# Two transformer blocks on one core: the fused loop's last stage with seven products on POOL, sums in four transfers, tokens turned a body ahead

## The chip, the cores and the metric

The kernel runs on one core of one Trainium2 chip. The metric is device time in microseconds, the median of several executions. In this text PE is the matmul engine (PEld its weight load), DVE the vector engine, ACT the scalar engine, POOL GpSimd, SP the engine that stores the output. Instructions of one engine run in the order in which they are written; engines wait for each other on semaphores.

## The reference

The input is 32 batches of 256 tokens with 128 features. Two blocks follow each other: causal attention with a mixture of experts, then hyperbolic attention with an MLP, each on a normalised input with a residual sum. The change lies in the second block alone:

```python
def _hyperbolic_distance(q, k, c):
    q_norm_sq = jnp.sum(q * q, axis=-1, keepdims=True)
    k_norm_sq = jnp.sum(k * k, axis=-1)[..., None, :]
    qk = jnp.einsum('bhnd,bhmd->bhnm', q, k)
    diff_sq = q_norm_sq + k_norm_sq - 2.0 * qk
    denom = (1.0 - c * q_norm_sq) * (1.0 - c * k_norm_sq)
    denom = jnp.maximum(denom, 1e-06)
    cosh_arg = 1.0 + 2.0 * c * diff_sq / denom
    cosh_arg = jnp.maximum(cosh_arg, 1.0)
    return jnp.arccosh(cosh_arg)
...
dist = _hyperbolic_distance(q, k, CURVATURE)     # 16 heads of 8 features
attn = jax.nn.softmax(-dist, axis=-1)
out = jnp.einsum('bhnm,bhmd->bhnd', attn, v)
return out @ wo.T
...
h = jax.nn.relu(jnp.einsum('bsd,dw->bsw', x, w1) + b1)   # the MLP, 512 wide
return jnp.einsum('bsw,wd->bsd', h, w2) + b2
```

## The kernel before

Three stages follow each other: causal attention, the mixture of experts, and the fused stage `hyperbolic_attention_and_mlp`, which has the change. The fused stage starts near 1343 us of the profiled execution and runs to the end. Its loop has one body per batch. In body b, every engine works on several batches at once: distances of batch b, softmax weights and values of batch b - 1, the back part of attention of batch b - 2, the residual and the normalisation for the MLP of batch b - 3, the MLP's products of batch b - 4 and b - 5, and the preparation of batch b + 1.

The 16 heads are taken in 8 pairs, and a body has 8 steps, one for each pair. For each pair:

- PE turns the pair's rows (`pe_turn_rows`, into `r_ps[p % 2]`), ACT (pairs 0 and 3) or DVE copies them to SBUF (`copy_rows`), and PE makes the pair products in `d_ps` and `i_ps` (`pe_pairs`). Both are single buffers, so PE makes those of the next pair only after DVE has read both.
- DVE reads `d_ps` (`dve_distances`), then `i_ps` (`dve_ratio`), and leaves u, a number from which the arccosh follows as log(1 + u + sqrt(u (u + 2))).
- For a pair in `PRODUCTS`, POOL makes u (u + 2) in `spare` (`pool_product`) and ACT takes one root. For the others, ACT takes two roots, of u/2 + 1 and of u/2 (`act_roots`).
- POOL issues a transfer that adds `spare` onto u (`pool_sum`).
- In the next body, ACT takes the logarithm and the exponential (`act_weights`), and PE multiplies with the values (`pe_values`).

The order on each engine is written out by hand in a function `body`. Step numbers in it (`VALUES_AT`, `BACK_AT`, `HIDDEN_AT` and so on) say in which step a piece stands. The first line of a step is the product of the following pair:

```python
for p in range(HP):
    following = next_pair(b, p, one_after)
    if following:
        pe_pairs(pe, *following, i if p + 1 < HP else (i + 1) % TURN)
```

`pe_keep_busy` issues matmuls whose output nobody reads; `BUSY_AHEAD` and `BUSY_BEHIND` say how many, and in which step. ACT loads one table for logarithm and exponential at the head of a body, and one for the roots behind the weights.

Of the kernel before, what the change touches and what calls it, by code (L numbers as in the profile page):

```python
# [12 lines left out]
ALU = mybir.AluOpType  # L13
# [1221 lines left out]
def hyperbolic_attention_and_mlp(nc, io, keep, y_dram, batches):  # L1235
# [11 lines left out]
    PRODUCTS = (0, 1, 2, 3, 4, 5)  # L1247
    SUMS_BEHIND = {5: (0, 1, 2, 3, 4, 5, 6, 7)}
# [5 lines left out]
    BUSY_AHEAD, BUSY_BEHIND = {5: 1}, {4: 4, 7: 1}  # L1254
    HW = WB // 2
    NORM_BEHIND, NORM4_BEHIND = 2, 5
    with ExitStack() as stack:
# [15 lines left out]
        twos = m.sb("twos", [P, 4])  # L1273
# [38 lines left out]
        sum_landed = [S_(f"sum_landed{n}") for n in range(HP)]  # L1312
# [9 lines left out]
        def wait_sum(engine, b, p):  # L1322

            after(engine, sum_landed[p], 16 * (b + 1))
# [12 lines left out]
        def pe_turn_x(pe, b):  # L1337
            pe.wait_ge(xh_done, (b + 1) * TB)
            after(pe, res_done, b - 3)
            after(pe, hi_done, b * TB)  # L1340
            after(pe, qkv_taken, b * TB)
            for j in range(TB):
                last = nc.tensor.transpose(misc[:, j * P:(j + 1) * P], xh[:, j, :], keep.ident)
            last.then_inc(xh_turned, 1)

        def pe_qkv(pe, b, j):
            pe.wait_ge(xT_done, b + 1)
            after(pe, hi_done, b * TB + j)
# [69 lines left out]

        def pe_keep_busy(count):
# [4 lines left out]
        def pe_fold_w1(pe):  # L1424
            pe.wait_ge(weights_in, 16 * 5)
            nc.tensor.matmul(o_ps[:, :], zsum[:, :], w1_rows[:, :], start=True, stop=False)
# [8 lines left out]
        def pe_hidden(pe, b, half, rows_read):  # L1435
            if half == 0:
                pe.wait_ge(w1_folded, 1)
# [27 lines left out]
        def act_xT(act, b):  # L1465
            act.wait_ge(xh_turned, b + 1)
            after(act, qkv_ready, b * TB)
            nc.scalar.copy(xTs[:, 0, :], misc[:, 0:N]).then_inc(xT_done, 1)

        def act_both_xT(act, b, b4):  # L1470
# [4 lines left out]
            nc.scalar.copy(xTs[:, :, :].rearrange("p s n -> p (s n)"), misc[:, :]).then_inc(xT_done, 1)  # L1475
# [69 lines left out]
        def pool_sum(pool, b, p, i):  # L1545
            pool.wait_ge(root_done, b * HP + p + 1)
            nc.gpsimd.dma_start(u[:, slot(i, p), :], spare[:, p, :], accum_op=ALU.add).then_inc(sum_landed[p], 16)  # L1547

        def pool_product(pool, b, p, i):
# [4 lines left out]
            nc.gpsimd.tensor_tensor(extra[:, 0:4], pair[:, 0:4], twos[:, :], ALU.add)  # L1554
            nc.gpsimd.tensor_scalar(extra[:, 4:2 * W2], pair[:, 4:2 * W2], 1.0, 2.0, ALU.mult, ALU.add).then_inc(raised, 1)  # L1555
# [149 lines left out]
        with nc.Block() as block:  # L1705
            @block.tensor
            def _(pe):
# [6 lines left out]
                pe_fold_w1(pe)  # L1714

                def body(b, i, one_before, two_before, three_before, four_before, five_before, one_after, two_after):
                    for p in range(HP):
# [30 lines left out]
                        if one_after:  # L1748
                            for r in {6: (2,), 7: (4,)}.get(p, ()):
                                pe_turn_rows(pe, b + 1, r)  # L1750
                        if one_before:
                            if p == HP - 1:
                                pe.wait_ge(o_copied, 2 * b)
                            pe_keep_busy(BUSY_BEHIND.get(p, 0))
                        if five_before and p == 0:
                            pe_y(pe, b - 5, 2 * (b - 1))
                        if four_before and p == HIDDEN_AT[0]:
                            if not one_after:
                                pe.wait_ge(late_xT4_done, 1)
# [46 lines left out]
            def _(act):  # L1806
# [284 lines left out]
```

## Time and profile before

| | us |
|---|---|
| median of 3 runs | 2449.32 (2448.59 to 2451.76) |
| profiled execution | 2456.33 |
| its span on the core | 2454.2 |
| PE, DVE, ACT, POOL busy in the span | 2089.9, 1956.8, 1767.4, 1627.2 |
| fused stage, from 1343.7 to the end | 1110.5 |
| in it DVE, ACT, POOL busy | 991.59, 1026.34, 1011.91 |

The shares of the whole span (85, 80, 72 and 66%) are means over three stages with different limits. The fused stage takes 1110.5 of the 2454.2 us, and only that part of the profile answers to the change.

### The profile page before, as it was taken

How to read it: one execution, taken by the hardware profiler on the slowest of the kernel's cores; microseconds unless marked ns; L12 is line 12 of the kernel's file. 1: busy time of each engine (PE TensorE's matmuls, PEld its weight loads, DVE VectorE, ACT ScalarE, POOL GpSimd, SP SyncE). 2: the span in 40 equal slices, each digit the busy share in tenths (PEclk: the TensorE clock that was granted, in tenths of full speed). 3: DMA queues.
4: the chain of work that ended last, by engine and by line, in shares of the span. 5: the costliest groups of instructions: out<-in, count | busy, mean ns of one | idle time of the engine just before them, and what ended most of it. 6: DMA issues, size and time to landing. Idle time of an engine off the chain costs nothing. (4 is left out here: it accounts for less than half of the span.)

```text
span 2454.2 us, 50808 instructions
## 1 busy us (share of the span) xinstructions
PE 2089.9 (85%) x15438; PEld 1566.8 (64%) x15438; DVE 1956.8 (80%) x5939; ACT 1767.4 (72%) x3085; POOL 1627.2 (66%) x1866
## 2 busy tenths in 40 slices
PE   4999999999999996999997677777777778777876
PEld 4677777777777775888885445555555555555554
DVE  4677776776777774778775899999999999999992
ACT  2666666666666762444432799999999999999996
POOL 2776676766666750000001899999999999999993
PEclk7999999999999996999997579888888988889888
DMA  5000000000000003353450466776666777666674
GB/s 142 1 2 2 2 1 2 2 1 2 1 2 1 2 2 70 86 119 76 96 114 10 93 127 130 139 138 128 124 119 127 141 141 134 119 129 124 129 142 80
DMA packets 81388, 184.24 MB, mean 75 GB/s; under 512 B 9479, under 2 KB 31530, under 8 KB 81195
## 3 DMA queue, kind: packets, MB, share of 16 engines
q0 software_dynamic: 36864, 134.23, 29.1%
q1 hardware_dynamic: 36010, 43.38, 7.9%
q10 hardware_dynamic: 8320, 4.19, 0.7%
q8 instruction: 103, 1.69, 0.3%
q14 instruction: 91, 0.74, 0.1%
HBM read 42.85 MB, written 4.72 MB: 19 GB/s over the span
## 5 line engine op out<-in xcount | busy, mean ns | idle before, releaser
L1557 POOL TENSOR_TENSOR spare<-spare,u 128x1024 f32<-128x1024 f32 x192 | 456.2, 2376 | 16.0
L542 ACT ACTIVATE prob<-s_ps,nmax 128x128 f32<-128x128 f32 (+1 forms) x1024 | 364.4, 432 | 132.2 <-DVE nmax L599 132.2
L599 DVE CUSTOM_DVE_ANT_0 s_ps<-s_ps,mask 128x128 f32<-128x128 f32 (+1 forms) x1024 | 340.7, 385 | 100.7 <-issue 76.4
L1633 DVE TENSOR_SCALAR u<-d_ps 128x1024 f32<-128x1024 f32 x256 | 312.1, 1219 | 48.7 <-PE i_ps L1374 48.1
L579 POOL TENSOR_TENSOR g_lo<-g_all,g_hi 128x512 fp32r<-128x512 f32 x256 | 329.1, 1286 | 21.4
L1637 DVE SCALAR_TENSOR_TENSOR u<-i_ps,u 128x1024 f32<-128x1024 f32 x256 | 313.5, 1225 | 13.2 <-DVE u L1633 0.5
L1374 PE MATMUL d_ps<-rowsT 28*128 28x256 f32 x1024 | 144.7, 357 | 149.5 <-DVE u L1637 145.9
L534 ACT COPY g_all<-g_ps 128x512 f32<-128x512 f32 x256 | 151.5, 592 | 162.6 <-PE g_ps L63 161.5
L1514 ACT ACTIVATE u<-u 128x1024 f32<-128x1024 f32 x256 | 257.0, 1056 | 1.7 <-DMA u<-spare 1.6
L1517 ACT ACTIVATE u<-u 128x1024 f32<-128x1024 f32 x256 | 255.7, 1051 | 0.0
L1374 PEld LDWEIGHTS d_ps<-rowsT 28*128 28x128 f32 x1024 | 92.4, 208 | 246.3 <-issue 241.7
L991 POOL TENSOR_TENSOR x_lo<-xTs,x_hi 128x512 fp32r<-128x512 f32 x16 | 21.9, 1372 | 326.8 <-ACT x_hi L987 326.8
L475 PE MATMUL t_ps<-ident,prob 128*128 128x128 f32 x1536 | 232.1, 274 | 1.6 <-ACT pT L609 1.2
L1547 POOL DMA_DIRECT2D u<-spare x256 | 228.5, 1447 | 2.0 <-ACT u L1506 1.2
L475 PEld LDWEIGHTS t_ps<-ident,prob 128*128 128x128 f32 x1536 | 192.0, 141 | 55.6 <-ACT prob L542 2.0
L1555 POOL TENSOR_SCALAR spare<-u 128x1020 f32<-128x1020 f32 x192 | 219.3, 1142 | 0.0
L1392 PE MATMUL o_ps<-u,v 128*32 128x256 f32 x2048 | 156.2, 428 | 69.9 <-ACT u L1517 69.4
L1362 PE MATMUL r_ps<-ident,rows 128*128 128x128 f32 x1024 | 186.2, 320 | 32.2 <-ACT rowsT L1494 26.4
L1159 ACT ACTIVATE act_g<-eg_ps 128x512 f32<-128x512 f32 x128 | 76.3, 598 | 189.7 <-PE eg_ps L63 189.7
L61 PE MATMUL s_ps<-g_hi,x_hi 128*128 128x512 f32 x384 | 188.6, 491 | 21.3 <-issue 17.5
L612 DVE COPY pT<-t_ps 128x512 f32<-128x512 f32 x256 | 176.7, 690 | 33.8 <-PE t_ps L475 27.5
L555 POOL TENSOR_TENSOR g_hi<-g_all,ones 128x4 fp32r<-128x4 f32 x256 | 51.6, 201 | 223.0 <-ACT g_all L534 219.5
(275 smaller groups left out, 5795.2 us busy)
## 6 DMA issues: line engine op xcount, KB each, us to landing
u<-spare POOLq DMA_DIRECT2D x256, 512.0 KB, 12.2
w_all<-w_rows SPq DMA_DIRECT2D x128, 256.0 KB, 5.9
x<-L_attn_x ACTq DMA_DIRECT2D x8, 512.0 KB, 13.9
y<-x SPq DMA_DIRECT2D x32, 128.0 KB, 10.0
wkqv<-L_attn_Wkqv SPq DMA_DIRECT2D x4, 528.0 KB, 8.9
gate_rows<-L_ffn_gate_proj SPq DMA_DIRECT2D x1, 512.0 KB, 14.4
up_rows<-L_ffn_up_proj SPq DMA_DIRECT2D x1, 512.0 KB, 11.1
down_cols<-L_ffn_down_proj SPq DMA_DIRECT2D x1, 512.0 KB, 13.0
```

Source lines behind the costliest of these rows:

```text
L475: last = nc.tensor.transpose(t_ps[s % 2][:, c * P:(c + 1) * P], prob[:, s % 3, c, :], keep.ident)
L542: last = nc.scalar.activation(prob[:, kind, at, :].rearrange("p c n -> p (c n)"), s_ps[kind][:, at.start * P:at.stop * P], ACT.Exp, bias=n ...
L579: nc.gpsimd.tensor_tensor(g_lo[:, gb, q, :], g_all[:, h % 2, :], g_hi[:, gb, q, :], ALU.subtract).then_inc(g_split, 1)
L599: last = nc.vector.tensor_tensor_reduce(out=scores, in0=scores, in1=keep.mask[:, N - width:N], scale=-1.0, scalar=3.4e38, op0=ALU.add, op1 ...
L1374: last = nc.tensor.matmul(ps[:, e * W2 + j * N:e * W2 + (j + 1) * N], rowsT[at, slot(i, p), 1, j * P:(j + 1) * P], rowsT[at, slot(i, p), 0 ...
L1514: nc.scalar.activation(pair, pair, ACT.Ln, bias=1.0 if whole else 0.0).then_inc(ln_done, 1)
L1517: nc.scalar.activation(pair, pair, ACT.Exp, scale=-1.0 if whole else -2.0).then_inc(w_done, 1)
L1547: nc.gpsimd.dma_start(u[:, slot(i, p), :], spare[:, p, :], accum_op=ALU.add).then_inc(sum_landed[p], 16)
L1555: nc.gpsimd.tensor_scalar(extra[:, 4:2 * W2], pair[:, 4:2 * W2], 1.0, 2.0, ALU.mult, ALU.add).then_inc(raised, 1)
L1557: nc.gpsimd.tensor_tensor(extra, extra, pair, ALU.mult).then_inc(prod_done, 1)
L1633: nc.vector.tensor_scalar(u[:, slot(i, p), :], d_ps[:, :], 0.0, None, ALU.max).then_inc(dist_done, 1)
L1637: nc.vector.scalar_tensor_tensor(out=u[:, slot(i, p), :], in0=i_ps[:, :], scalar=1.0 / DEN_MIN, in1=u[:, slot(i, p), :], op0=ALU.min, op1= ...
```

## The change

On POOL, `PRODUCTS` gets pair 6 as a seventh product, and the product is made of two instructions of full width where it had three (4 columns, 1,020 columns, 1,024 columns). The sums go in four transfers of two pairs each (1 MB) where there were eight of one pair: pairs 0 and 1 behind product 5, pairs 2 to 5 behind product 6 and the MLP's normalisation (`pool_norm4`), and pairs 6 and 7 behind product 0 of the following body. On DVE, the features of the next batch move from step 4 to step 5, and the MLP's addition (`dve_y`) from step 1 to step 2. On ACT, the second relu stands between the logarithms and the exponentials of pairs 4 and 5. On PE, rows are turned one step later or behind another piece, the tokens of attention and MLP are turned at the end of the preceding body into `o_ps` (before: into `misc` at step 0), a wait for ACT's copy of them stands at step 0, and of the unread products one goes at step 7 and four come at step 5.

```diff
-    PRODUCTS = (0, 1, 2, 3, 4, 5)
-    SUMS_BEHIND = {5: (0, 1, 2, 3, 4, 5, 6, 7)}
+    PRODUCTS = (0, 1, 2, 3, 4, 5, 6)
+    SUMS_BEHIND = {5: (0,), 6: (2, 4)}
...
-    BUSY_AHEAD, BUSY_BEHIND = {5: 1}, {4: 4, 7: 1}
+    FEATURES_AT = 5
+    BUSY_BESIDE = {5: 4}
+    BUSY_AHEAD, BUSY_BEHIND = {5: 1}, {4: 4}
     HW = WB // 2
-    NORM_BEHIND, NORM4_BEHIND = 2, 5
+    NORM_BEHIND, NORM4_BEHIND = 2, 6
...
         def pe_turn_x(pe, b):
             pe.wait_ge(xh_done, (b + 1) * TB)
-            after(pe, res_done, b - 3)
-            after(pe, hi_done, b * TB)
-            after(pe, qkv_taken, b * TB)
+            after(pe, xT_done, b)
             for j in range(TB):
-                last = nc.tensor.transpose(misc[:, j * P:(j + 1) * P], xh[:, j, :], keep.ident)
+                last = nc.tensor.transpose(o_ps[:, j * P:(j + 1) * P], xh[:, j, :], keep.ident)
...
+        def pe_keep_busy_beside(pe, b, count):
+            after(pe, relu_done, 2 * (b - 4) + 1)
+            after(pe, rowsT_done[0], (b + 1) * (HP // 2))
+            for n in range(count):
+                nc.tensor.matmul(r_ps[0][:, 0:N], keep.ident, keep.qkvoT[:, 0:2, :], start=True, stop=True,
+                                 skip_group_check=True)
...
         def pool_sum(pool, b, p, i):
-            pool.wait_ge(root_done, b * HP + p + 1)
-            nc.gpsimd.dma_start(u[:, slot(i, p), :], spare[:, p, :], accum_op=ALU.add).then_inc(sum_landed[p], 16)
+            pool.wait_ge(root_done, b * HP + p + 2)
+            at = slot(i, p)
+            nc.gpsimd.dma_start(u[:, at:at + 2, :], spare[:, p:p + 2, :], accum_op=ALU.add).then_inc(sum_landed[p // 2], 16)
...
-            nc.gpsimd.tensor_tensor(extra[:, 0:4], pair[:, 0:4], twos[:, :], ALU.add)
-            nc.gpsimd.tensor_scalar(extra[:, 4:2 * W2], pair[:, 4:2 * W2], 1.0, 2.0, ALU.mult, ALU.add).then_inc(raised, 1)
+            nc.gpsimd.tensor_scalar(extra, pair, 1.0, 2.0, ALU.mult, ALU.add).then_inc(raised, 1)
...
-                        if one_after and p == 0:
-                            pe_turn_x(pe, b + 1)
-                        if four_before and p == 0:
-                            if not one_after:
-                                pe.wait_ge(res_done, b - 2)
-                            pe_turn_x4(pe, b - 4, (i - 4) % TURN, misc, N)
...
-                            for r in {5: (0,), 6: (1,), 7: (3,)}.get(p, ()):
+                            for r in {6: (0,), 7: (2, 3)}.get(p, ()):
                                 pe_turn_rows(pe, b + 1, r)
...
-                            for r in {6: (2,), 7: (4,)}.get(p, ()):
+                            for r in {6: (1,), 7: (4,)}.get(p, ()):
                                 pe_turn_rows(pe, b + 1, r)
+                        if p == HP - 1 and one_after:
+                            if one_before:
+                                pe.wait_ge(o_copied, 2 * b)
+                            if two_after:
+                                pe_turn_x(pe, b + 2)
+                            if three_before:
+                                pe_turn_x4(pe, b - 3, i, o_ps, N)
...
+                        if four_before and one_after and p in BUSY_BESIDE:
+                            pe_keep_busy_beside(pe, b, BUSY_BESIDE[p])
+                        if p == 0 and one_after:
+                            pe.wait_ge(xT_done, b + 2)
...
-                def weights(b, i, p):
-                    for logarithm in (True, False):
-                        for n in range(2):
-                            act_weights(act, b, p + n, i, logarithm)
+                def weights(b, i, p, relu_of=None):
+                    for n in range(2):
+                        act_weights(act, b, p + n, i, True)
+                    if relu_of is not None:
+                        act_relu(act, relu_of, 1)
+                    for n in range(2):
+                        act_weights(act, b, p + n, i, False)
...
                     for p in PRODUCTS:
                         pool_product(pool, b, p, i)
+                        if p == 0 and one_before:
+                            pool_sum(pool, b - 1, HP - 2, (i - 1) % TURN)
                         if p == NORM_BEHIND and two_after:
                             pool_norm(pool, b + 2)
+                        if p == NORM4_BEHIND and three_before:
+                            pool_norm4(pool, b - 3, i)
                         for n in SUMS_BEHIND.get(p, ()):
                             pool_sum(pool, b, n, i)
-                            if n == NORM4_BEHIND and three_before:
-                                pool_norm4(pool, b - 3, i)
...
-                        if p == 1 and five_before:
+                        if p == 2 and five_before:
                             dve_y(dve, b - 5)
...
-                            if p == 4:
+                            if p == FEATURES_AT:
                                 after(dve, relu_done, 2 * (b - 3))
                                 dve_features(dve, b + 1)
                                 dve_features_end(dve, b + 1)
```

The order of rows shows three places of it. The first is PE's from step 6 to step 7, here in the last body but one (`L1362` turns four blocks of rows, `L1409` the attention output, `L1374` makes the pair products). Before:

```order
3516 L1362 MATMUL r_ps<-ident,rows 128x128 [waits rowsT_done1]
3517 L1362 MATMUL r_ps<-ident,rows 128x128 x3
3518 L1409 MATMUL misc<-ident,attn 128x128 [waits attn_done3]
3519 L1409 MATMUL misc<-ident,attn 128x128
3520 L1362 MATMUL r_ps<-ident,rows 128x128 [waits rowsT_done0]
3521 L1362 MATMUL r_ps<-ident,rows 128x128 x3
3522 L1374 MATMUL d_ps<-rowsT 128x256 [waits u_done,dist_done,rowsT_done0]
```

The same place of the change, where `L1363` turns rows and `L1375` makes the pair products:

```order
3525 L1363 MATMUL r_ps<-ident,rows 128x128 [waits rowsT_done1]
3526 L1363 MATMUL r_ps<-ident,rows 128x128 x3
3527 L1375 MATMUL d_ps<-rowsT 128x256 [waits u_done,dist_done,rowsT_done0]
3528 L1375 MATMUL d_ps<-rowsT 128x256
3529 L1375 MATMUL i_ps<-rowsT 128x256 x2
3530 L1375 MATMUL d_ps<-rowsT 128x256 x2
3531 L1375 MATMUL i_ps<-rowsT 128x256 x2
3532 L1363 MATMUL r_ps<-ident,rows 128x128 [waits rowsT_done0]
3533 L1363 MATMUL r_ps<-ident,rows 128x128 x3
```

Rows 2, the pair that waits for `rowsT_done0` above, stood ahead of the first pair of the next body and stand behind it now.

The second is DVE's step 4. The copy of `o_ps` and three small instructions on `misc` follow the ratio, then the features (from TENSOR_REDUCE on). Before:

```order
2446 L1637 SCALAR_TENSOR_TENSOR u<-i_ps,u 128x1024
2447 L1668 BN_AGGR part_mv<-part_stats 128x2 x2
2448 L1643 COPY o<-o_ps 128x512
2449 L1582 SCALAR_TENSOR_TENSOR rows<-misc,rows 128x16x8
2450 L1584 TENSOR_TENSOR rows<-misc,rows 128x16x8
2451 L1585 COPY v<-misc 128x16x8
2452 L1589 TENSOR_REDUCE r_ps<-sq 128x64
```

The same place of the change:

```order
2446 L1644 SCALAR_TENSOR_TENSOR u<-i_ps,u 128x1024
2447 L1675 BN_AGGR part_mv<-part_stats 128x2 x2
2448 L1650 COPY o<-o_ps 128x512
2449 L1589 SCALAR_TENSOR_TENSOR rows<-misc,rows 128x16x8
2450 L1591 TENSOR_TENSOR rows<-misc,rows 128x16x8
2451 L1592 COPY v<-misc 128x16x8
2452 L1640 TENSOR_SCALAR u<-d_ps 128x1024
2453 L1644 SCALAR_TENSOR_TENSOR u<-i_ps,u 128x1024
2454 L1596 TENSOR_REDUCE r_ps<-sq 128x64
```

The distances and the ratio of pair 5 now stand ahead of the features.

The third is POOL's turn from one body to the next (`spare<-u` and `spare<-spare,u` are a product, `xh<-x` and `x<-x,biases` the MLP's normalisation, DMA a transfer). Before:

```order
1094 L1554 TENSOR_TENSOR spare<-u,twos 128x4
1095 L1555 TENSOR_SCALAR spare<-u 128x1020
1096 L1557 TENSOR_TENSOR spare<-spare,u 128x1024
1097 L1547 DMA u<-spare 128x1024 x6
1098 L1570 TENSOR_SCALAR xh<-x,part_mv,rstd 128x127 x2
1099 L1574 TENSOR_TENSOR x<-x,biases 128x256
1100 L1547 DMA u<-spare 128x1024 x2
1101 L1554 TENSOR_TENSOR spare<-u,twos 128x4
```

The same place of the change:

```order
1001 L1562 TENSOR_SCALAR spare<-u 128x1024
1002 L1564 TENSOR_TENSOR spare<-spare,u 128x1024
1003 L1555 DMA u<-spare 128x2048
1004 L1562 TENSOR_SCALAR spare<-u 128x1024
1005 L1564 TENSOR_TENSOR spare<-spare,u 128x1024
1006 L1577 TENSOR_SCALAR xh<-x,part_mv,rstd 128x127 x2
1007 L1581 TENSOR_TENSOR x<-x,biases 128x256
1008 L1555 DMA u<-spare 128x2048 x2
1009 L1562 TENSOR_SCALAR spare<-u 128x1024
1010 L1564 TENSOR_TENSOR spare<-spare,u 128x1024
1011 L1555 DMA u<-spare 128x2048
```

Four transfers of 2,048 columns stand where eight of 1,024 did, and the last of them is behind the first product of the next body.

## Rows read from the trace of the kernel before

**Rows 1.** Busy time by stage: us, PE, PEld, DVE, ACT, POOL, clock, DMA.

```profile
1574.30:2373.30 799.00, 619.43 (x5234) 426.84 (x5232) 748.99 (x1465) 769.42 (x985) 759.62 (x743) 0.89 0.69 130
```

**Rows 2.** Timeline of ACT, head of two bodies: start, us, engine, line.

```profile
1941.39 1.28 ACT L1824 ACT_TABLE_LOAD   x1
...
1973.76 1.28 ACT L1824 ACT_TABLE_LOAD   x1
```

**Rows 3.** PE by slices of 1 us: length, busy, granted clock, DMA, GB/s.

```profile
1967.79:1968.79 1.00, 0.48 (x4) 1.00 1.02 197
...
1969.79:1970.79 1.00, 1.00 (x10) 0.50 0.98 172
```

**Rows 4.** Waits from 1574.3 to 2373.3: us in total, times, longest.

```profile
DVE u L1633 <- PE i_ps L1374: 28.2, 60, 1.8
...
ACT hidden L1542 <- PE r_ps L1442: 13.8, 24, 0.8
ACT xTs L1475 <- PE misc L1432: 11.9, 12, 1.4
```

**Rows 5.** Timeline of ACT, five roots.

```profile
1930.59 4.83 ACT L1501 ACTIVATE spare<-spare 128x1024 f32<-128x1024 f32 x5
```

**Rows 6.** Timeline of POOL, one product and the start of the next.

```profile
1947.07 0.20 POOL L1554 TENSOR_TENSOR spare<-u,twos 128x4 f32<-128x4 f32 x1
1947.23 1.04 POOL L1555 TENSOR_SCALAR spare<-u 128x1020 f32<-128x1020 f32 x1
...
1950.70 0.20 POOL L1554 TENSOR_TENSOR spare<-u,twos 128x4 f32<-128x4 f32 x1
```

**Rows 7.** Groups of instructions, 1574.3 to 2373.3: busy us, mean ns | idle before.

```profile
L1547 POOL DMA_DIRECT2D u<-spare x192 | 171.4, 1441 | 0.5 <-issue 0.3
```

**Rows 8.** Line of the transfers from 1960 to 1980, with landing.

```profile
L1547 POOL DMA_DIRECT2D u<-spare x8: 901/1351/2217, 1966.2 to 1974.6; - x8
...
DMA to landing us min/median/max: 4.8/12.7/15.4
```

**Rows 9.** Timeline of DVE, one body: ratios (L1637), distances (L1633), row copies.

```profile
1939.41 1.23 DVE L1637 SCALAR_TENSOR_TENSOR u<-i_ps,u 128x1024 f32<-128x1024 f32 x1
...
1950.30 1.23 DVE L1637 SCALAR_TENSOR_TENSOR u<-i_ps,u 128x1024 f32<-128x1024 f32 x1
...
1952.32 1.23 DVE L1633 TENSOR_SCALAR u<-d_ps 128x1024 f32<-128x1024 f32 x1 [0.40 <-PE i_ps L1374]
...
1961.28 1.23 DVE L1637 SCALAR_TENSOR_TENSOR u<-i_ps,u 128x1024 f32<-128x1024 f32 x1
...
1963.44 1.22 DVE L1633 TENSOR_SCALAR u<-d_ps 128x1024 f32<-128x1024 f32 x1 [0.44 <-PE i_ps L1374]
1964.70 1.22 DVE L1637 SCALAR_TENSOR_TENSOR u<-i_ps,u 128x1024 f32<-128x1024 f32 x1
...
1968.42 1.22 DVE L1637 SCALAR_TENSOR_TENSOR u<-i_ps,u 128x1024 f32<-128x1024 f32 x1
1969.56 1.28 DVE L1494 CAST rowsT<-r_ps 128x512 fp32r<-128x512 f32 x2
1970.75 1.22 DVE L1633 TENSOR_SCALAR u<-d_ps 128x1024 f32<-128x1024 f32 x1
```

**Rows 10.** Timeline of PE: unread products, pair products, turned rows.

```profile
1928.11 2.05 PE L1421 MATMUL o_ps<-qkvoT,ident 128*128 128x256 f32 x8
...
1933.55 0.38 PE L1374 MATMUL d_ps<-rowsT 28*128 28x256 f32 x2
...
1933.99 0.66 PE L1362 MATMUL r_ps<-ident,rows 128*128 128x128 f32 x4
...
1951.67 0.38 PE L1374 MATMUL d_ps<-rowsT 28*128 28x256 f32 x2 [1.30 <-DVE u L1637]
...
1969.79 0.58 PE L1374 MATMUL d_ps<-rowsT 28*128 28x256 f32 x2 [0.82 <-DVE u L1637]
...
1970.52 1.11 PE L1362 MATMUL r_ps<-ident,rows 128*128 128x128 f32 x4
```

More of the change, by code:

```diff
@@ L1311, in hyperbolic_attention_and_mlp @@
         prod_done, root_done, ln_done, w_done, pv_done = S_("prod_done"), S_("root_done"), S_("ln_done"), S_("w_done"), S_("pv_done3")
-        sum_landed = [S_(f"sum_landed{n}") for n in range(HP)]
+        sum_landed = [S_(f"sum_landed{n}") for n in range(HP // 2)]
         o_copied, o_turned, rec_done, attn_done = S_("o_copied3"), S_("o_turned3"), S_("rec_done3"), S_("attn_done3")
@@ L1322, in wait_sum @@
         def wait_sum(engine, b, p):
-            after(engine, sum_landed[p], 16 * (b + 1))
+            after(engine, sum_landed[p // 2], 16 * (b + 1))
         def slot(i, p):
@@ L1347, in pe_qkv @@
             pe.wait_ge(xT_done, b + 1)
+            if j == 0:
+                after(pe, res_done, b - 3)
             after(pe, hi_done, b * TB + j)
@@ L1425, in pe_fold_w1 @@
             pe.wait_ge(weights_in, 16 * 5)
+            pe.wait_ge(xT_done, 1)
             nc.tensor.matmul(o_ps[:, :], zsum[:, :], w1_rows[:, :], start=True, stop=False)
@@ L1435, in pe_hidden @@
         def pe_hidden(pe, b, half, rows_read):
-            if half == 0:
-                pe.wait_ge(w1_folded, 1)
             pe.wait_ge(rowsT_done[half], rows_read)
@@ L1467, in act_xT @@
             after(act, qkv_ready, b * TB)
-            nc.scalar.copy(xTs[:, 0, :], misc[:, 0:N]).then_inc(xT_done, 1)
+            nc.scalar.copy(xTs[:, 0, :], o_ps[:, 0:N]).then_inc(xT_done, 1)
         def act_both_xT(act, b, b4):
@@ L1474, in act_both_xT @@
             after(act, h_ready, 2 * b4)
-            nc.scalar.copy(xTs[:, :, :].rearrange("p s n -> p (s n)"), misc[:, :]).then_inc(xT_done, 1)
+            nc.scalar.copy(xTs[:, :, :].rearrange("p s n -> p (s n)"), o_ps[:, :]).then_inc(xT_done, 1)
         def act_hi(act, b, j):
@@ L1714, in _ @@
                 pe_fold_w1(pe)
+                pe.wait_ge(w1_folded, 1)
+                pe_turn_x(pe, 1)
                 def body(b, i, one_before, two_before, three_before, four_before, five_before, one_after, two_after):
@@ L1748, in body @@
                         if one_after:
-                            for r in {6: (2,), 7: (4,)}.get(p, ()):
+                            for r in {6: (1,), 7: (4,)}.get(p, ()):
                                 pe_turn_rows(pe, b + 1, r)
+                        if p == HP - 1 and one_after:
[5 more added lines that the diff above has]
+                                pe_turn_x4(pe, b - 3, i, o_ps, N)
                         if one_before:
-                            if p == HP - 1:
-                                pe.wait_ge(o_copied, 2 * b)
                             pe_keep_busy(BUSY_BEHIND.get(p, 0))
+                        if four_before and one_after and p in BUSY_BESIDE:
+                            pe_keep_busy_beside(pe, b, BUSY_BESIDE[p])
+                        if p == 0 and one_after:
+                            pe.wait_ge(xT_done, b + 2)
+                        if p == 0 and not one_after:
+                            pe.wait_ge(late_xT4_done, 1)
                         if five_before and p == 0:
@@ L1830, in body @@
                     elif four_before:
-                        act_late_xT4(act, b - 4, misc[:, N:2 * N])
+                        act_late_xT4(act, b - 4, o_ps[:, N:2 * N])
                     for p in range(0, HP, 2):
                         if one_before:
-                            weights(b - 1, (i - 1) % TURN, p)
+                            weights(b - 1, (i - 1) % TURN, p, b - 4 if four_before and p == 4 else None)
                         if one_after and p in (0, 2):
@@ L1837, in body @@
                         if four_before and p == 2:
-                            for half in range(2):
-                                act_relu(act, b - 4, half)
+                            act_relu(act, b - 4, 0)
                     if three_before:
@@ L1888, in body @@
                         pool_product(pool, b, p, i)
+                        if p == 0 and one_before:
+                            pool_sum(pool, b - 1, HP - 2, (i - 1) % TURN)
                         if p == NORM_BEHIND and two_after:
                             pool_norm(pool, b + 2)
+                        if p == NORM4_BEHIND and three_before:
+                            pool_norm4(pool, b - 3, i)
                         for n in SUMS_BEHIND.get(p, ()):
                             pool_sum(pool, b, n, i)
-                            if n == NORM4_BEHIND and three_before:
-                                pool_norm4(pool, b - 3, i)
                 written_out(body)
+                pool_sum(pool, END, HP - 2, END % TURN)
                 for b in (END - 2, END - 1, END):
                     pool_norm4(pool, b, b % TURN)
-                for p in range(HP):
+                for p in range(0, HP, 2):
                     wait_sum(pool, END, p)
```

5 lines of the change are left out of this document (removed).

## The prediction

> **What bounds the kernel now.** I read the fused loop in its stage table, then each engine's row order inside one body, then the waits. The loop's 24 even bodies take 799.00 us [rows 1], so 33.29 us a body. Per body DVE is busy 748.99/24 = 31.21 us, ACT 769.42/24 = 32.06, POOL 759.62/24 = 31.65. Nothing has a microsecond and a half to spare, so what matters is the order. The starts of the table load at the head of ACT's body show what a clean body takes: 1941.39 to 1973.76 is 32.37 us [rows 2]. The mean lies 0.9 us above it, so other bodies are longer. I call this the loss of the long bodies. The clock rows show what goes with them: TensorE is 0.48 busy in the slice before the fall with 1.00 granted, and then 1.00 busy with 0.50 granted, the lower of its two levels [rows 3], just where the last pair of a body and the first of the next are made.
>
> Waits of all 24 bodies [rows 4]: DVE for PE's pair products 28.2 us (1.18 a body), ACT for the hidden products 13.8 (0.58), ACT for the turned tokens 11.9 (0.50). I number steps 0 to 7 after the pair whose ratio DVE makes.
>
> **The change part by part.**
>
> ACT. Pair 6 becomes a product on POOL, so its two roots become one. Five roots take 4.83 us, 0.95 apart [rows 5]. 32.06 - 0.95 = 31.1. The second relu goes between the logarithms and exponentials of pairs 4 and 5, and tokens are turned a body ahead, so that the waits of 0.58 and 0.50 go as well. ACT stops being a bound: 31.1 against 33.29. I count nothing for this by itself; DVE then decides.
>
> POOL. A product goes from 1947.07 to the next at 1950.70, 3.63 us, and 0.16 of it is the 4-column instruction that goes (1947.07 to 1947.23) [rows 6]. The full width adds 4 columns to 1,020, which cannot be seen. So: 31.65 - 6 x 0.16 + 3.47 = 34.16 before transfers. The 192 transfer issues keep POOL busy 171.4 us, 0.89 each [rows 7]. Four of them go: if an issue costs by the transfer, POOL falls to 34.16 - 3.57 = 30.6; if it costs by the byte, four doubled ones cost 1.79 each and POOL stays at 34.2. No row has a row of 8 KB, so both ends stay in. I take the lower: the row pattern stays one run per partition, and what is made is a list of runs.
> The Trainium skill ("DMA: Bandwidth & Descriptors", The descriptor swizzle) has 8 data descriptors per engine for 1 MiB to 128 partitions, one per partition, which gives the 30.6; the same page (SDMA does more than copy) puts 2,048 elements as the most that an adding descriptor takes, exactly this size, and a cut below it would give the 34.2. No run here shows either.
>
> The transfers themselves. Eight land between 1966.2 + 4.8 = 1971.0 and 1974.6 + 15.4 = 1990.0 [rows 8], 2.71 us each; a doubled one takes 5.4 and the first lands 4.8 + 2.7 = 7.5 after its issue. Bytes are the same. I count a body from the start of ratio 0. Ratio 6 starts at 1964.70 - 1939.41 = 25.29 [rows 9], 0.44 less after the change (step 5 below), and lasts 1.2: product 6 runs from 26.1 to 29.6. The MLP's normalisation behind it takes about 2.4 (an estimate from its place among the transfers), so the transfers of pairs 2 to 5 go out at 32.0 and land at 39.5 and 44.9; that of pairs 6 and 7, issued behind product 0 of the next body at 37.6, lands at 50.3, which is 17.4 into the next body of 32.9. ACT: root 6 at 29.6, two roots of pair 7, a row copy, so its next body starts at 33.0, or 0.1 of the next body, where it started at 1941.39 - 1939.41 = 1.98. Its table load, token copy, 12 activations of 0.95, the copies and relus between them make 15.8 (estimate), so it asks at 15.9 and waits 1.5; at the end it again waits for product 6, so this costs nothing. It is the tightest of the waits that the change adds; behind it on ACT queue all roots. On POOL the two transfers and the next product 0 stand behind the MLP's normalisation, on PE the turn of the MLP's tokens waits for it: it is there near 31.5, PE asks at 32.7. Hidden.
>
> DVE and PE. DVE's work is the same, only its order changes. From the start of a ratio to the pair products is 1.37 us (1950.30 to 1951.67), to the next distances 2.02 (1952.32, 0.40 of it waited) [rows 9, 10]. Whatever DVE has behind the ratio hides this if it reaches 0.88 us.
> - Step 5 now: ratio 1961.28, distances 1963.44, 0.44 waited [rows 9]. The features (some 4 us by the number of small instructions, all in a row) move here, so the wait goes: -0.44. Step 4 keeps a copy and three small ones, enough cover.
> - DVE's MLP addition goes from step 1 to 2: both keep enough cover. Nothing.
> - Step 7: before, rows 2 were turned ahead of the first pair of the next body; now behind it, since rows 0 come a step later. DVE copies rows 1 and 2 there: ratio 1968.42, copies 1969.56, distances 1970.75, 2.33 us [rows 9]. Now the second copy must wait: 1.37 to the pair products, 0.44 till PE goes on to rows (1933.55 to 1933.99), 0.66 for them, 0.04 to DVE = 2.51, and 0.62 for the copy: 3.13. That is +0.80. At the lower clock the same two are 0.73 (1969.79 to 1970.52) and 1.11 [rows 10]: 3.25 + 0.62, +0.74 more.
> - At step 0 PE now waits for ACT's copy of the tokens before the MLP's second product; queued behind is pair 2, for which DVE waits. The copy ends about 2 us into ACT's body, and ACT now starts it 1.9 us earlier than before. Hidden; without the lead it would cost 0.4.
> - Unread products: eight records take 2.05 us [rows 10], four products. Four are added at step 5, one goes at step 7. PE has 2.5 us idle in step 5: nothing on the path. What they do to the clock is the open question.
>
> Clean body: 32.4 - 0.44 + 0.80 = 32.76 us. Loss of the long bodies: 0.89 before. Step 7 no longer ends with an unread product behind a slow clock and ACT no longer holds PE's values at step 4, but PE has little to do between the added products and pair 7 and again before step 7. Bounds: none, to 1.2 in each body (0.74 at step 7 and about 0.45 at step 0). I take 0.27, 33.03. Some 28 bodies run this way: (33.03 - 33.29) x 28 = -7.3. The last body ends with a doubled transfer and a later product 6, of which I leave +1. Against the profiled execution of 2456.3 (span 2454.2) this is 2450.0; the runs shown have their median 7.0 below that execution, so 2449.3 - 6.3 = 2443.0.
>
> **The rivals.**
> - The clock falls in every body at steps 6 and 7 (slower). Place: the rows turned behind the first pair. Price 0.74 to 1.2 on 32.76, body 33.5 to 34.0, +6 to +20, and +1: 2456 to 2470. It decides once the mean loss is above 0.53 (33.29 - 32.76). For it: 2.0 us of PE work in step 6's 3.7 and an idle stretch on each side. Against: denser step 5 and step 7. 0.22.
> - The two cancel, loss 0.45 to 0.7: 2446 to 2453. 0.14.
> - The wait at step 7 is no wait (DVE comes late there anyway, or other work slips in) and the clock holds: 32.4 - 0.44 + 0.3 = 32.3, (32.3 - 33.29) x 28 = -28: 2422, at best 2418. For it: ACT and POOL both get a microsecond of slack. Against: PE's order, which leaves rows 2 behind the pair. 0.12.
> - Issues cost by the byte, or the doubled transfers land late: POOL 34.2 and its small gaps, body 34.3 to 34.6, +28 to +37: 2477 to 2486. 0.10.
> - Forecast as above, loss 0 to 0.45: 2435 to 2447. 0.42.
>
> **How the numbers follow.** 0.2% is 4.9 us, about what a measurement of this kernel can tell. Forecast: 0.34 faster, 0.08 within. With 0.12 faster by more: 0.46. Within: 0.08 + 0.14 = 0.22. Slower: 0.22 + 0.10 = 0.32. The range leaves out the costly issues (0.10), the top of the clock case (0.05) and the lowest edge (0.03): 2425 to 2464.
>
> **What would show it.** In the profile after: POOL busy near 30.6 a body and 0.9 per issue, or 34 with 1.8. ACT near 31.1 and no wait of its relu or of its token copy; it waits for product 6 instead. DVE idle 0.4 at step 3, none at step 5, and a new wait of 0.7 to 0.8 before the second row copy of step 7, ended by PE's rows. Table loads 32.8 apart where the clock stays at 1.00. Wrong if that row copy does not wait, if logarithms of pairs 6 and 7 wait for a transfer by over 2 us, or if the granted clock at steps 6 and 7 is 0.50 in most bodies.

## The result and the profile after

| | us |
|---|---|
| before, median of 12 runs | 2449.18 (2444.56 to 2451.76) |
| the change, median of 12 runs | 2454.99 (2450.29 to 2463.32) |
| ratio, 95% interval | 1.0024 (1.0013 to 1.0034) |
| forecast | 2443.0 (2425 to 2464) |

The change makes the kernel slower by a quarter of a per cent. The time lies in the range, but on the other side of before than forecast. It lies between two rivals: the one in which gain and loss cancel (2446 to 2453) and the one in which the granted clock falls and eats the gain (2456 to 2470).

The stage table over the same 799 us as [rows 1]:

```profile
sum 799.00, PE 627.09 PEld 444.58 DVE 742.04 ACT 747.86 POOL 728.40; mean PE 627.09 PEld 444.58 DVE 742.04 ACT 747.86 POOL 728.40
```

The length of a body follows from the table loads at the head of ACT's body, 31 of them. I call a body clean when no fall of the granted clock to 0.50 lengthens it. The first load, the end of a clean body, and the last load (timeline of ACT):

```profile
1373.96 1.28 ACT L1839 ACT_TABLE_LOAD   x1
...
2344.18 1.28 ACT L1839 ACT_TABLE_LOAD   x1
...
2377.74 1.28 ACT L1839 ACT_TABLE_LOAD   x1
```

The load before 2344.18 stands at 2311.46, so a clean body takes 32.72 us. The mean is (2377.74 - 1373.96)/30 = 33.46; before it is 33.26 by the same rule. 799.00/33.46 makes 23.9 bodies, and in each DVE is busy 31.07, ACT 31.32, POOL 30.50 us. POOL and ACT did become lighter (31.65 and 32.06 before). The waits of the stage, against [rows 4]:

```profile
POOL u L1555 <- ACT spare L1508: 26.8, 24, 2.7
...
DVE rowsT L1501 <- PE r_ps L1363: 21.2, 23, 1.5
DVE u L1640 <- PE i_ps L1375: 20.3, 34, 1.3
```

The last two are what DVE waits for. Its wait for pair products went from 28.2 to 20.3 us, and a wait for turned rows of 21.2 is new. It stands at step 7 (timeline of DVE, step 7 of a clean body):

```profile
2306.71 1.22 DVE L1644 SCALAR_TENSOR_TENSOR u<-i_ps,u 128x1024 f32<-128x1024 f32 x1
2307.85 0.68 DVE L1501 CAST rowsT<-r_ps 128x512 fp32r<-128x512 f32 x1
2309.30 0.69 DVE L1501 CAST rowsT<-r_ps 128x512 fp32r<-128x512 f32 x1 [0.77 <-PE r_ps L1363]
2309.91 1.21 DVE L1640 TENSOR_SCALAR u<-d_ps 128x1024 f32<-128x1024 f32 x1
```

From ratio to distances it takes 3.20 us, where it was 2.33 [rows 9]. The rest of the loss is not in a clean body. PE at step 0, in a body where the clock falls (2078) and in one where it holds (2345): turned rows, then the MLP's second product, then the products of pair 2.

```profile
2078.45 1.70 PE L1363 MATMUL r_ps<-ident,rows 128*128 128x128 f32 x8
2079.95 3.02 PE L1460 MATMUL o_ps<-w,hidden 128*128 128x128 f32 x16
2082.90 0.39 PE L1375 MATMUL d_ps<-rowsT 28*128 28x256 f32 x2
...
2345.84 1.09 PE L1363 MATMUL r_ps<-ident,rows 128*128 128x128 f32 x8
2346.77 1.95 PE L1460 MATMUL o_ps<-w,hidden 128*128 128x128 f32 x16
2348.71 0.39 PE L1375 MATMUL d_ps<-rowsT 28*128 28x256 f32 x2
```

The granted clock of such stretches (windows of 1 us of PE: length, busy, granted clock, DMA, GB/s):

```profile
2079.83:2080.83 1.00, 1.00 (x7) 0.50 1.20 246
...
2346.18:2347.18 1.00, 1.00 (x11) 1.00 1.02 197
```

And DVE behind the slow one, where pair 2 comes late:

```profile
2083.55 1.22 DVE L1640 TENSOR_SCALAR u<-d_ps 128x1024 f32<-128x1024 f32 x1 [1.17 <-PE i_ps L1375]
```

A table worked out from DVE's timeline makes the account: the time from one ratio to the next, by step, as a mean over 25 or 26 whole bodies of a profile, which leaves out the loop's first ones, and for a clean body.

```
step                       0     1     2     3     4     5     6     7    body
before, clean            3.32  3.92  3.65  3.35  7.62  3.28  3.63  3.58  32.36
before, mean             3.71  4.23  3.65  3.35  7.63  3.49  3.68  3.58  33.33
before_again, mean       3.71  4.16  3.65  3.35  7.63  3.41  3.68  3.58  33.18
the change, clean        3.32  3.58  3.99  3.35  3.71  6.78  3.54  4.45  32.72
the change, mean         3.34  4.03  3.98  3.36  3.72  6.81  3.61  4.58  33.43
change_again, mean       3.34  3.63  3.98  3.35  3.71  6.79  3.58  4.64  33.03
```

Between the clean rows, steps 4 to 6 give 0.50 us back and step 7 takes 0.87; steps 1 and 2 only exchange the MLP's addition. The means lie above the clean rows where the clock falls: at steps 0 and 1 before (4.2 and 4.4 in about every third body), at step 1 (4.85) or step 7 (5.20) after. A fall at the end of step 4 adds a little at step 5 before (3.42 for 3.28).

### The profile page after: what moved, and what is told of

Read it like the earlier page. It is cut to its first block and busy times, and to the rows that moved or that the text cites. A ratio compares the mean times of both kernels' runs of the same rounds, so it can differ in the third digit from the quotient of the medians.

```text
span 2461.5 us, 50910 instructions
## 1 busy us (share of the span) xinstructions
PE 2101.2 (85%) x15592; PEld 1593.8 (65%) x15592; DVE 1952.3 (79%) x5939; ACT 1742.9 (71%) x3053; POOL 1589.3 (65%) x1609
## 3 DMA queue, kind: packets, MB, share of 16 engines
q0 software_dynamic: 18432, 134.23, 27.1%
## 5 line engine op out<-in xcount | busy, mean ns | idle before, releaser
L1564 POOL TENSOR_TENSOR spare<-spare,u 128x1024 f32<-128x1024 f32 x224 | 530.8, 2370 | 18.7
L1375 PE MATMUL d_ps<-rowsT 28*128 28x256 f32 x1024 | 137.1, 342 | 181.0 <-DVE u L1644 180.2
L1562 POOL TENSOR_SCALAR spare<-u 128x1024 f32<-128x1024 f32 x224 | 244.8, 1093 | 59.0 <-DVE u L1644 58.8
L1375 PEld LDWEIGHTS d_ps<-rowsT 28*128 28x128 f32 x1024 | 87.4, 197 | 269.9 <-issue 265.6
L1508 ACT ACTIVATE spare<-spare 128x1024 f32<-128x1024 f32 x224 | 222.5, 1047 | 11.8 <-POOL spare L1564 11.5
L1393 PE MATMUL o_ps<-u,v 128*32 128x256 f32 x2048 | 149.5, 412 | 46.4 <-ACT u L1524 34.2
L1363 PE MATMUL r_ps<-ident,rows 128*128 128x128 f32 x1024 | 179.6, 319 | 5.9 <-DVE rows L1635 5.7
```

The lines of the kernel that those rows point to most:

```text
L1363: last = nc.tensor.transpose(r_ps[p % 2][:, at:at + P], src, keep.ident)
L1375: last = nc.tensor.matmul(ps[:, e * W2 + j * N:e * W2 + (j + 1) * N], rowsT[at, slot(i, p), 1, j * P:(j + 1) * P], rowsT[at, slot(i, p), 0 ...
L1562: nc.gpsimd.tensor_scalar(extra, pair, 1.0, 2.0, ALU.mult, ALU.add).then_inc(raised, 1)
L1564: nc.gpsimd.tensor_tensor(extra, extra, pair, ALU.mult).then_inc(prod_done, 1)
```

## The experiments

Theory A is that a body is the sum of DVE's steps at the full clock plus what the lower clock adds. It follows that the change lost by the place of rows 2. The ratios below are to before, each from its own runs.

**Rows 2 ahead of the first pair, on the change.**

```diff
-for r in {6: (0,), 7: (2, 3)}.get(p, ()):
+for r in {6: (0,), 7: (3,)}.get(p, ()):
...
-for r in {6: (1,), 7: (4,)}.get(p, ()):
+for r in {6: (1, 2), 7: (4,)}.get(p, ()):
```

> The change with one thing taken back: rows 2 are turned in step 6, ahead of the first pair of the next body. Theory A (the body is the sum of DVE's steps at the full clock, 32.72 us, plus what the lower clock adds at steps 7, 0 and 1, 0.7 a body so far): step 7 falls from 4.45 to about 3.6 us, the clean body to 31.85, and with a loss between 0 and 1.3 the kernel takes 2407 to 2446, so 9 to 48 us less than the changed kernel's 2455. Theory B (POOL's and ACT's new waits set the body, the row copy's wait is only slack): the wait of 0.9 turns up at another place of DVE and the time stays within 3 us of 2455.

Measured 2425.65 us, ratio 0.9904 (0.9883 to 0.9924): about 29 us below the change. Step 7 of DVE, timeline:

```profile
2205.32 1.23 DVE L1644 SCALAR_TENSOR_TENSOR u<-i_ps,u 128x1024 f32<-128x1024 f32 x1
2206.46 1.28 DVE L1501 CAST rowsT<-r_ps 128x512 fp32r<-128x512 f32 x2
2207.65 1.21 DVE L1640 TENSOR_SCALAR u<-d_ps 128x1024 f32<-128x1024 f32 x1
```

It takes 2.33 us again, the shortest bodies 31.82, the mean of 30 bodies 32.42. Theory B, which forecast no change of the time, is out. This version beats both kernels. PE here waits for ACT's copy of the tokens at step 0, the wait that the prediction named and called hidden:

```profile
PE o_ps L1460 <- ACT xTs L1482: 6.7, 14, 1.0
```

**Rows 2 behind the first pair, on the kernel before.** `{7: (2, 3)}` where it had `{7: (3,)}` and `{6: (2,)}`.

> The kernel before with one thing added: rows 2 are turned behind the first pair of the next body. Theory A: step 7 grows from 3.58 to 4.45 us, the clean body from 32.37 to 33.24; if the loss by the lower clock stays at 0.89 a body the kernel takes 2449 + 26 = 2475, if the clock happens to hold 2449 to 2455. Theory B: ACT and POOL leave no room to hide it either, so it is 2475 there too; if it is hidden, 2449. It mostly sizes the term alone.

Measured 2480.02 us, ratio 1.0122 (1.0108 to 1.0137). The second copy waits here as it does in the change (timeline of DVE):

```profile
2017.01 0.68 DVE L1494 CAST rowsT<-r_ps 128x512 fp32r<-128x512 f32 x1
2018.46 0.69 DVE L1494 CAST rowsT<-r_ps 128x512 fp32r<-128x512 f32 x1 [0.77 <-PE r_ps L1362]
```

The body grows by 0.86 to 34.12 us. Taken back or added, this one line of order is worth 1.2% of the time (0.9904/1.0024, and 1.0122).

**More unread products at step 6, on the change.** Four at the end of step 6, behind a wait for the copy of `o_ps`.

```diff
-BUSY_AHEAD, BUSY_BEHIND = {5: 1}, {4: 4}
+BUSY_AHEAD, BUSY_BEHIND = {5: 1}, {4: 4, 6: 4}
```

> The change with four more unread products at the end of step 6, where PE is idle for 1.4 to 1.8 us. Theory A, where the lower clock is what separates the measured 33.46 us of a body from 32.75: if these products keep the granted clock up at steps 7, 0 and 1, all bodies take 32.7 to 32.9 and the kernel 2433 to 2440; if the clock falls all the same, they take 2 us each time there, delay pair 0, and it is 2455 to 2470. The trace tells which. Theory B: nothing, 2455.

Measured 2446.95 us, ratio 0.9995 (0.9981 to 1.0009). Step 1 falls from 4.03 to 3.69 and step 7 from 4.58 to 4.48 in the mean (the second profile of the change, below, has 3.63 and 4.64 with no edit). They hold the clock up in more bodies, not in all (three of the last 22 still have a fall at step 1), so it gave back half of what was expected or less.

**Without the four unread products of step 5, on the change.** `BUSY_BESIDE = {}`.

> The change without the four unread products of step 5. Theory A: they have no part in the clean body, which stays 32.7; the granted clock falls more often at steps 6 to 1, so the loss grows from 0.7 to between 1.0 and 1.4 a body and the kernel to 2464 to 2476. Rival C, the four products move the fall of the clock to the place where it costs most (step 1, where the MLP's second product stands ahead of pair 2), so without them the kernel gets faster, 2440 to 2450.

Measured 2457.37 us, ratio 1.0039 (1.0026 to 1.0052), not clear of the change's own interval. Step 1 has its clean 3.59 us, and step 7 takes 5.07 in the mean. So in the first profile of the change the four products had shifted the fall from step 7 to step 1 (rival C has this right), where it costs more each time but comes in fewer bodies. In its second profile one body has it at step 1. Nothing is gained by leaving them out, and neither forecast was met.

**The MLP's second product in two halves, on the change.** 8 matmuls at step 0, 8 late in step 1, ahead of the hidden products.

> The change with the MLP's second product (16 matmuls, 1.95 us at the full clock, 3.02 at the lower) cut in two: 8 of them at step 0 as now, 8 at the end of step 1. Theory A: what a fall of the clock costs is that these 16 stand ahead of pair 2, so step 1 takes 4.85 instead of 3.59 us in those bodies (0.45 a body in the mean of the changed kernel). With half of them there the fall costs at most 0.4 each: the mean of step 1 goes to 3.6 to 3.75, the kernel to 0.3 to 0.5% below the changed kernel, if the clock doesn't fall in other places. Rival D: step 1 has no room for 8 more (its own PE work is 2.7 us, 3.7 with them), so step 2 waits 0.1 to 0.5 in every body and the kernel is level with the change or slower.

Measured 2452.40 us, ratio 1.0018 (1.0009 to 1.0027), inside the change's own interval. The profile has step 1 at 3.62 instead of 4.03, and step 2 stays 3.98, so rival D's wait didn't come. But change_again below has 3.63 with no edit. What half a product is worth can't be told from this.

**Both, on the change.**

> Both edits on the change: rows 2 turned ahead of the first pair, and the second product cut in two. Theory A: clean body 31.85, the loss at step 1 (0.32 a body with rows 2 ahead alone) mostly gone: body 31.95 to 32.2, ratio to before 0.980 to 0.988. Rival E: at 31.9 us a body ACT (31.3 busy) and POOL (30.5) have no room left, their waits appear and the body stays at 32.3 or above: ratio 0.989 to 0.992.

Measured 2430.99 us, ratio 0.9925 (0.9910 to 0.9940), no better than rows 2 ahead alone. The mean body is 32.39, as rival E forecast, but not in its way: ACT, at 769.86/(799/32.39) = 31.2 us a body, does not hold every body. In DVE's timeline, with the loop's first body as body 0, step 5 takes 7.99 and 8.31 us in bodies 5 and 6 and 9.34 in body 30, the last but one, but 6.78 or 6.79 in each of the bodies 10 to 29. These 20 take 31.97 us in the mean, 0.13 above the shortest. (The same 20 with rows 2 ahead alone take 32.17.) What is left over is in the loop's first ten bodies and its end; which wait starts it there is not shown.

**Eight transfers at the places of the four, on the change.**

```diff
-            after(engine, sum_landed[p // 2], 16 * (b + 1))
+            after(engine, sum_landed[p // 2], 32 * (b + 1))
...
-            nc.gpsimd.dma_start(u[:, at:at + 2, :], spare[:, p:p + 2, :], accum_op=ALU.add).then_inc(sum_landed[p // 2], 16)
+            for n in range(2):
+                nc.gpsimd.dma_start(u[:, at + n, :], spare[:, p + n, :], accum_op=ALU.add).then_inc(sum_landed[p // 2], 16)
```

> The change with eight transfers of one pair at the places of the four, with the same bytes. If an issue costs by the transfer (0.9 us each) POOL's busy time goes from 30.5 to about 34.1 us a body and POOL becomes the bound: body 34.1 to 34.6, ratio to before 1.025 to 1.04. If the four larger ones had saved nothing, POOL would stay at 30.5 and the time within 0.2% of the changed kernel; the profile of the change already speaks against this, the run sizes what four transfers are worth.

Measured 2501.12 us, ratio 1.0221 (1.0206 to 1.0236), a little under the forecast ratio. The group of the issues here and in the change (busy us, mean ns | idle before):

```profile
L1556 POOL DMA_DIRECT2D u<-spare x184 | 163.7, 1183 | 0.5 <-ACT spare L1508 0.3 <-issue 0.2
```

```profile
L1555 POOL DMA_DIRECT2D u<-spare x96 | 85.8, 960 | 27.8 <-ACT spare L1508 26.8 <-ACT u L1513 0.8 <-issue 0.2
```

0.89 us each in both, at half and at double size. POOL is busy 783.25/(799/34.70) = 34.0 us a body and bounds it. With seven products, four transfers are worth 2%. The pages' queue rows, before and the change (packets, MB, share), show how a transfer of double size is made:

```profile
q0 software_dynamic: 36864, 134.23, 29.1%
q0 software_dynamic: 18432, 134.23, 27.1%
```

256 transfers have 36,864 packets and 128 have 18,432, so 144 each at either size, and the bytes are the same. So the rows of 8 KB are not cut.

**POOL's part alone, on the kernel before.** `PRODUCTS` with pair 6, products of two instructions, four transfers, the normalisation behind product 6.

> The kernel before with POOL's part of the change alone: seven products of two instructions, four transfers, the MLP's normalisation behind product 6 (ACT then takes one root for pair 6). Theory A: DVE and PE keep their order, which sets the body, so the time stays within 0.3% of before, although ACT loses 0.95 us of work and POOL 1 us. Rival F: in before ACT and POOL have part in the loss of the long bodies, and the slack gives 0.3 to 0.8 us a body, ratio 0.990 to 0.996.

Measured 2453.18 us, ratio 1.0022 (1.0008 to 1.0036). The body is 33.14 us, against 33.26 and 33.11 in the two profiles of before: no gain from a lighter POOL and ACT. The end behind the last table load takes 86.5 us where before took 81.0; in it ACT waits 2.12 us for the last transfer.

**ACT's copy ahead of its table load, with rows 2 ahead.** The call of `act_both_xT` stands in front of `preload_act_table_set`.

> The change with rows 2 turned ahead of the first pair and, new, ACT's copy of the turned tokens ahead of its table load of 1.28 us. With rows 2 ahead alone, PE's second MLP product waited for that copy in 14 bodies of the stretch, 6.7 us in all and up to 1.0, with pair 2 queued behind. Theory A: the copy ends 1.3 us sooner, the wait goes, the mean of step 1 falls from 3.90 to between 3.6 and 3.75, ratio to before 0.983 to 0.989. Rival E (ACT and POOL are the bound now, by the landing of the last transfer: ACT waits 11.1 us for it in that stretch): it stays at 0.989 to 0.992.

Measured 2426.13 us, ratio 0.9915 (0.9901 to 0.9930). The wait for the copy is gone and step 1 is at its clean 3.59, but steps 5 and 6 take 6.92 and 3.73 in the mean. Step 5 grows in bodies 6, 8 and 16 (9.12, 7.52, 7.02) and at the end of the loop alone. ACT's waits for a transfer grow:

```profile
ACT u L1521 <- DMA u<-spare: 18.2, 32, 2.0
```

They were 2.9 us in the change. In the profile the body is 32.23, 0.19 less; the medians don't show it.

**The same with two unread products at step 6, and the same without those of step 5.**

> The same with two more unread products between rows 1 and rows 2 at step 6. Theory A: as in busy_at_6 the granted clock falls less often at steps 7 to 1; with rows 2 ahead it falls there in few bodies anyway, so the gain is at most 0.2% over the kernel without them; PE has 0.26 + 0.88 us idle there at the full clock, so nothing is lost. Rival: at the lower clock they delay pair 0 and the kernel is 0.1 to 0.3% slower.

> Rows 2 ahead, the copy first, and without the four unread products of step 5. If their place in the change's cost is only to shift where the clock falls (with rows 2 behind they moved the loss from step 7 to step 1 at nearly the same time), leaving them out here puts the fall on steps 7 and 0, and costs 0 to 0.4%; if they hold the clock, 0.5 to 1%.

Measured 2425.41 us, ratio 0.9914 (0.9899 to 0.9930), and 2424.28 us, ratio 0.9913 (0.9897 to 0.9929). With rows 2 in their place, neither kind of unread product shows in the time.

**The features back at step 4, on the change.** `FEATURES_AT = 4`.

> The change with the features back at step 4, all else as in it. This sizes the term of 0.44 us that I gave the move: step 5's wait of 0.4 for the pair products returns, steps 4 to 6 take 14.5 instead of 14.0 us, and the kernel 0.3 to 0.6% more than the changed one, ratio to before 1.005 to 1.009. Rival: the second relu, which ACT now makes later, holds the features at step 4 and it costs 1% or more; or the clock shifts and hides the 0.44.

Measured 2490.86 us, ratio 1.0167 (1.0142 to 1.0192), three times the expected price. Step 5's wait is back (steps 4 and 5 take 10.93 for 10.49 us), and step 6 takes at least 4.29 instead of 3.53. Pair 7 stands on PE behind the eight unread products (timeline of PE, then of DVE):

```profile
2009.40 1.89 PE L1424 MATMUL r_ps<-qkvoT,ident 128*128 128x256 f32 x8
2011.23 0.39 PE L1375 MATMUL d_ps<-rowsT 28*128 28x256 f32 x2
```

```profile
2011.79 1.23 DVE L1640 TENSOR_SCALAR u<-d_ps 128x1024 f32<-128x1024 f32 x1 [0.67 <-PE i_ps L1375]
```

**The same without the unread products of step 5.**

> The change with the features at step 4 and without the four unread products of step 5. With both edits the 0.67 us for which DVE waited at step 6 in features_at_4 (pair 7 queued behind the unread products) should go, and only the wait of step 5 be left: 0.3 to 0.44 us a body over no_beside, ratio to before 1.007 to 1.011. Rival: the wait at step 6 has another cause (ACT's values or the turned tokens), and it stays near 1.0167.

Measured 2482.23 us, ratio 1.0129 (1.0106 to 1.0152). Step 6 is back at 3.5 to 3.7 in 21 of 26 bodies, so that wait was the unread products'. The shortest body is 33.12, 0.40 above the change's clean one, which is the term of the features. But the mean of 30 bodies is 34.11: the clock falls at step 1 (4.7 to 5.0 us) in 7 bodies, at step 6 (5.05) in 5 and at step 7 in others. The clean term was right, the price came from the clock again.

**Both kernels once more.**

> The changed kernel once more, unedited, for a second profile. The first profile is of its slowest execution (2463.3 against a median of 2455.0). If the loss by the lower clock (0.74 us a body in that profile) is a property of the order, it is between 0.5 and 0.8 here too; if it is the scatter of one execution, it may be 0.3 to 0.5, and the clean body 32.72 in both. Ratio to before 1.001 to 1.004.

> The kernel before once more, unedited, for a second profile: clean body 32.37, mean 33.0 to 33.3, so a loss of 0.6 to 0.9.

The change measured 2454.19 us, ratio 1.0021 (1.0008 to 1.0034), before in one run 2448.82. These profiles are of executions close to the medians. The first, the fourth and the last table load of the change, then of before:

```profile
1374.39 1.28 ACT L1839 ACT_TABLE_LOAD   x1
...
1475.14 1.28 ACT L1839 ACT_TABLE_LOAD   x1
...
2367.81 1.28 ACT L1839 ACT_TABLE_LOAD   x1
```

```profile
1372.30 1.28 ACT L1824 ACT_TABLE_LOAD   x1
...
1469.81 1.28 ACT L1824 ACT_TABLE_LOAD   x1
...
2365.68 1.28 ACT L1824 ACT_TABLE_LOAD   x1
```

Both mean bodies are 33.11 us. With the clean bodies of 32.72 and 32.36 the loss by the clock is 0.39 in the change and 0.75 before, where the first profiles gave 0.74 and 0.90. The spans differ by 5.0 us: 2.1 ahead of the first load, nothing in the 30 bodies, 2.9 behind the last (84.0 against 81.1).

That nothing is two parts. The first three bodies from the first load on (bodies 1 to 3, counted from 0) take 100.75 us in the change and 97.51 before, the other 27 take 33.06 and 33.18 each: 3.2 us lost and 3.2 won. In the first pair of profiles the first three take 100.83 and 98.28, the other 27 take 33.44 and 33.32. The loss of the first three is again step 7. In both profiles of the change it takes 5.11 us in bodies 2 and 3, where before takes 3.59 (4.45 is the clean step of the change). The granted clock is down there, as the window of PE (length, busy, granted clock, DMA, GB/s) shows beside the wait of the second row copy:

```profile
1472.50:1473.65 1.15, 1.15 (x10) 0.50 0.11 21
...
1473.65 0.69 DVE L1501 CAST rowsT<-r_ps 128x512 fp32r<-128x512 f32 x1 [1.43 <-PE r_ps L1363]
```

The unread products of step 5 don't run yet in these bodies (their condition is `four_before`). With rows 2 ahead, step 7 takes 3.58 us there and the first three bodies take 95.77.

## Why the prediction was right and wrong

- **Clean body: right.** 32.76 forecast, 32.72 measured. Step 5's wait went (0.44 forecast; 0.50 over steps 4 to 6). Step 7 was forecast +0.80 and came at +0.87, by the mechanism named: rows 2 stand behind the pair on PE, the second row copy waits. Two experiments, one in each kernel, confirm it.
- **POOL and ACT: right.** 30.6 and 31.1 forecast, 30.50 and 31.32 measured. An issue costs by the transfer, 0.89 us at either size. That agrees with what I took from the Trainium skill ("DMA: Bandwidth & Descriptors", The descriptor swizzle), one data descriptor per partition. The same page's most of 2,048 elements (SDMA does more than copy) does not cut this transfer: it has 144 packets at either size. That ACT and POOL don't set the body in this order is shown by before_seven.
- **The loss of the long bodies: the step that failed.** I set 0.89 before against 0.27 after, a gain of 0.62 a body, which outweighed the +0.36 of the clean body, and took it for 28 bodies: -7.3 us. Over the 30 bodies the loss is 0.90 and 0.74 in the first profiles, 0.75 and 0.39 in the second. The gain is 0.16 to 0.36 a body, and the clean body's +0.36 eats it: +0.20 or 0.00 us a body, where I had -0.26. Three errors are in it. The 0.89 was read from an execution 7 us above its median, and one near it has 0.75, so part of the gain did not exist. The first three bodies don't run like the others: together they lose 2.6 and 3.2 us, by the lower clock at step 7 on top of the rows' new place. And the price of a fall was set too low in the first profile of the change: 0.74 at step 7 was right (5.20 against 4.45), but for the stretch behind it I had 0.45, and at step 1 it is 1.27, since the rows and the 16 matmuls of the MLP's second product (+0.61 and +1.07 us at the lower clock) stand ahead of pair 2 in PE's queue. That profile has 9 such bodies of 26. The second has one, and its loss is at step 7.
- **The unread products.** I left open what they do to the clock. Those of step 5 shift the fall from step 7 to step 1 in one profile of the change and thin it out at step 7 in the other (4.64 against 5.07 without them); the time without them is the same within the intervals. With four more at step 6, and falls in few bodies, it is 0.3% less.
- **The end of the loop: too small.** I left +1, and it is 2.8 and 2.9 in the two pairs of profiles. In a late MLP product of the change, the last but one, the clock falls, and it takes 3.44 us (3.53 in the second profile) where before's took 1.95, which is 1.5 of it. ACT waits 1.2 to 1.5 us there for a transfer and 0.7 for the last product, which it does not before; whether this makes the rest is not shown.

```profile
2450.63 3.44 PE L1460 MATMUL o_ps<-w,hidden 128*128 128x128 f32 x16
```

- **Waits called hidden.** That for ACT's copy at step 0 is hidden in the change, as forecast, and appears as soon as the body is 0.9 us shorter. For the last transfer I had 1.5 us of ACT in each body; it is 2.9 in 24 bodies, and product 6 costs ACT 4.9.

Added up, a pair's difference is the part ahead of the loop, the first three bodies, the other 27 and the end. In the first pair of profiles it is -1.44 + 2.55 + 3.38 + 2.78 = 7.27 us, in the pair near the medians 2.09 + 3.24 - 3.20 + 2.89 = 5.02. The two parts that nearly keep their size are the first three bodies and the end, 5.3 and 6.1 us together, where I had about +1; the medians differ by 5.8. The 27 bodies, from which I forecast the gain, have either sign. How much of the rest is the execution and how much the kernel stays open: the fall of the clock differs from one execution to the next, and I have two profiles of each. That the change is slower rests on the intervals of 12 runs, twice.

The change thus holds a gain and a loss. With seven products, four transfers, the features at step 5 and the tokens turned ahead it is 0.8 to 1.0% faster than before once rows 2 are turned in step 6.

## What to carry to other kernels

Work out the clean body first, step by step on the engine that binds: it came out within 0.04 us here and named the one line of order that was worth 1.2%. Keep what the clock adds as a term of its own, take it from more than one execution, count the first bodies of a loop and its end by themselves, and price a fall by everything that stands ahead of the awaited matmuls in PE's queue at the lower clock, not by the awaited ones alone. When a change bundles many moves, ask of each row that is turned or copied in advance whether it still stands ahead of the product that the next engine waits for.

## What was not expected of the hardware

The falls lock onto the loop. In the first profile of the change six bodies running, from 1940.6 to 2145.0, have their fall at the same two places, late in step 0, where it costs, and late in step 4, where it doesn't, and take 34.00 to 34.11 us each, while in the second profile of the same kernel one body has a fall that costs at step 1. Before has the same three bodies in turn for part of its first profile and half of its second, one long and two short (33.92, 32.48, 32.59 from ratio to ratio in the first). So a body's mean can differ by 0.35 us between executions of one program, though all its clean steps agree within 0.02 us. The first table load of the loop stood anywhere from 1357.7 to 1378.4 us in these profiles, though nothing in the two stages ahead was edited.
